# Decoder layer on one core: k's product in two halves around the closing scores, attended rows normalised two tiles at a time

## The chip, the cores and the metric

The kernel runs on one core of a Trainium2 chip. The metric is the time of one execution in microseconds (us), taken on the device. The names of the profile are used throughout: PE is TensorE's matmuls and PEld its weight loads, DVE is VectorE, ACT is ScalarE, POOL is GpSimd, SP is SyncE with its DMA queue. Each engine works through its own list of instructions in order. The engines meet only in semaphores: an instruction adds to one when it is done, and another engine waits until it has reached a count.

## The reference, cut to what matters

```python
# x: [128 sequences, 64 tokens, 128 features], 16 heads of 8 features
x = _layernorm(x + attn(x))            # linear attention and a quantised MLP
x = _layernorm(x + xattn(x, ctx))      # cross attention, the part that the change touches
x = _layernorm(x + ffn(x))             # shared and expert products, top-2 gate

def xattn(x, encoder_output, mask, WQ, WK, WV, WO):
    q = (x @ WQ).reshape(b, s, H, DK).transpose(0, 2, 1, 3)
    k = (encoder_output @ WK).reshape(b, s, H, DK).transpose(0, 2, 1, 3)
    v = (encoder_output @ WV).reshape(b, s, H, DK).transpose(0, 2, 1, 3)
    scores = jnp.einsum('bhqd,bhkd->bhqk', q, k) / SQRT_DK
    scores = jnp.where(masked_or_future, NEG, scores)
    attn = jax.nn.softmax(scores, axis=-1)
    ctx = jnp.einsum('bhqk,bhkd->bqhd', attn, v).reshape(b, s, d)
    return ctx @ WO
```

All of it is float32.

## The kernel before, in words

The 8192 tokens are 64 tiles of 128 rows, in 16 groups of four (`TG` = 4). Three phases follow one another, each a software pipeline over the groups, written out by hand for every engine: linear attention (`phase1`), the MLP (`phase2`), and cross attention with the gated products (`phase3`). The change is in `phase3`. No scheduler and no planner moves anything: the order in an engine's list is the order in which Python calls the helpers.

A step `s` of `phase3` has four slots, `t` = 0 to 3, one for each tile n = 4s + t of group s. Beside that, a step prepares group s + 1 (k, q and v of the context, copied and spread over heads) and finishes group s - 1 (projection of the attended rows, residual, norm, gated products).

What PE does in slot 0, in this order: it transposes tile n's probabilities; does the last gated product of group s - 2; transposes the attended rows of group s - 1 and the x rows of group s + 1; opens the scores of tiles n + 2 and n + 3 (`scores_open`, L1383 and L1394: half of the heads); multiplies tile n's probabilities with v (`weigh_values`, L1455 for an even tile, L1439 and L1446 for an odd one, all into PSUM bank 7); closes the scores of n + 2 and n + 3 (`scores_close`, the same two lines L1383 and L1394, the other half of the heads); and makes k of group s + 1 (`project_qk`, L1464 with `cT,w_xk`, one product of 128x512 into bank 5). Slot 1 follows with the transposes of tile n + 1 (L1427), the projection of the attended rows of group s - 1 (L1229), the q product (L1464 with `yT,w_xq`) and the odd tile's `weigh_values`. Slot 2 begins with transposes and the v product (L1475) and opens the next two tiles' scores.

`scores_close` in slot 0 waits for DVE: the opened half of tile n + 2 must have been read for its maxima (`opened_maxima`, L1040). `scores_open` in slot 2 waits for ACT's copy of the turned probabilities (L793) and for DVE's subtraction of tile n + 3's maxima (L1063), because it writes over the banks that both read.

What DVE does: in slot 0 `opened_maxima`, then `xattend` of tile n (L1030, the reciprocal of 16 sums, and L1032, the product with 128 values). In slot 1 it takes the maxima of the closed half (L1053), subtracts (L1070, two instructions), adds the projection of group s - 1 to x (`residual`, L1127), takes its statistics (L305, L312), and does tile n + 3's maxima and subtraction (L1057, L1063), then `xattend` of tile n + 1. Slots 2 and 3 have one `xattend` each.

`weigh_values` of every tile writes the same columns of bank 7, so it waits on `xatt_ready` until DVE has read the tile before.

## Time and profile before

| what | value |
|---|---|
| time, median of 3 runs (lowest to highest) | 551.51 us (551.32 to 553.45) |
| the profiled execution's own time | 551.02 us |
| its span | 549.3 us |
| busy, share of the span | PE 90%, PEld 67%, DVE 74%, ACT 64%, POOL 68% |

The span is what the profiler covers; the execution's own time is a little more than it. A busy share is an average over the three phases. The page's slices show PE at nine tenths or more in nearly all of the span, and DVE rising from 7 to 8 tenths in the second half, which is `phase3`. TensorE's granted clock is at full speed until the last two slices.

### The profile page before, as it was taken

To read this page: it belongs to the slowest core of one execution; us is meant where nothing else is said; L and a number is where in the kernel's file an instruction comes from. 1 tells how busy PE (TensorE), PEld (TensorE's weight loads), DVE (VectorE), ACT (ScalarE), POOL (GpSimd) and SP (SyncE) were. 2 spreads that over 40 slices of the span, in tenths; PEclk is the share of its full clock that TensorE was granted. 3 is DMA by queue.
4 is the path that set the end of the run, shared out by engine and by line. 5 is a ranking of instruction groups with operands and counts; after the bars stand their busy time and mean duration, and the time that the engine had idled before them with its cause. 6 is when DMAs were issued, how large, how long until landed. Compare 5 with 4: busy or idle time off the path is not lost. (4 is left out here: it accounts for less than half of the span.)

```text
span 549.3 us, 23033 instructions
## 1 busy us (share of the span) xinstructions
PE 495.5 (90%) x9328; PEld 369.2 (67%) x9328; DVE 405.0 (74%) x1410; ACT 354.2 (64%) x649; POOL 372.7 (68%) x685
## 2 busy tenths in 40 slices
PE   2899999998999999998799999999999999999870
PEld 1777777775777777775566767767676666767660
DVE  2777777765777677737577888878888888888866
ACT  1566666656777776764866777666776666767641
POOL 6566666645568785642254888887888878888744
PEclk9999999999999999999999999999999999999987
DMA  6630000000000000001110101211012110120001
GB/s 170 173 118 2 3 2 1 4 2 1 2 0 2 1 2 1 2 2 30 32 33 4 50 8 49 51 51 28 28 52 51 51 31 25 51 51 24 23 2 58
DMA packets 24746, 17.44 MB, mean 32 GB/s; under 512 B 2112, under 2 KB 22464, under 8 KB 24640
## 3 DMA queue, kind: packets, MB, share of 16 engines
q1 hardware_dynamic: 24208, 15.90, 10.5%
q8 instruction: 74, 1.21, 0.9%
q14 instruction: 32, 0.26, 0.1%
q10 hardware_dynamic: 432, 0.07, 0.1%
HBM read 11.77 MB, written 4.19 MB: 29 GB/s over the span
## 5 line engine op out<-in xcount | busy, mean ns | idle before, releaser
L793 ACT ACTIVATE gel<-pair 128x1024 f32<-128x1024 f32 x64 | 51.8, 809 | 40.4 <-PE pair L1427 39.3
L786 ACT ACTIVATE gel<-gel,row_scale 128x512 f32<-128x512 f32 x96 | 66.1, 723 | 18.0 <-DVE gel L1070 15.3
L1369 PEld LDWEIGHTS pair<-w,gel 128*128 128x128 f32 x512 | 60.4, 192 | 8.0 <-issue 5.7
L1369 PE MATMUL pair<-w,gel 128*128 128x128 f32 x512 | 62.5, 276 | 1.0 <-ACT gel L719 1.0
L536 POOL TENSOR_SCALAR k_exp<-k_sb,quad_mask 128x512 f32<-128x512 f32 x64 | 43.2, 694 | 26.9 <-ACT k_sb L766 18.1
L1333 PE MATMUL pair<-hT,w 128*128 128x512 f32 x128 | 58.3, 595 | 1.3 <-ACT lev L714 1.3
L1427 PE MATMUL pair<-ident,gel 128*128 128x128 f32 x384 | 55.3, 280 | 1.5 <-ACT gel L786 1.5
L1427 PEld LDWEIGHTS pair<-ident,gel 128*128 128x128 f32 x384 | 43.3, 141 | 18.4 <-issue 13.5
L1057 DVE TENSOR_REDUCE neg_max<-pair 128x16 f32<-128x512 f32 (+1 forms) x48 | 41.0, 854 | 5.5 <-PE pair L1394 5.5
L1394 PE MATMUL pair<-k_exp,qT 32*32 32x128 f32 (+1 forms) x2048 | 44.3, 333 | 0.0
L513 POOL TENSOR_TENSOR X<-X,proj_sb 128x512 f32<-128x512 f32 x16 | 20.4, 1272 | 35.4 <-ACT proj_sb L677 35.4
L1070 DVE TENSOR_TENSOR gel<-pair,neg_max 128x512 f32<-128x512 f32 x64 | 41.2, 686 | 1.1
L1224 PE MATMUL pair<-ident,xn 128*128 128x128 f32 x192 | 30.5, 283 | 9.6 <-POOL xn L344 9.4
L1333 PEld LDWEIGHTS pair<-hT,w 128*128 128x128 f32 x128 | 22.9, 190 | 24.0 <-issue 23.5
L321 POOL TENSOR_SCALAR veps_b<-mv_b 128x4 f32<-128x4 f32 (+1 forms) x33 | 7.7, 233 | 44.0 <-DVE mv_b L312 25.3
L719 ACT ACTIVATE gel<-lev 128x512 f32<-128x512 int8 x64 | 36.3, 619 | 0.9 <-DVE lev L972 0.9
L1224 PEld LDWEIGHTS pair<-ident,xn 128*128 128x128 f32 x192 | 23.8, 146 | 19.1 <-issue 17.3
L323 POOL TENSOR_TENSOR rstd_b<-veps_b,minus_half 128x4 f32<-128x4 f32 (+1 forms) x33 | 34.5, 1044 | 2.8
L305 DVE BATCH_NORM_STATS2 stats<-X 128x6 f32<-128x128 f32 x128 | 27.6, 279 | 10.5 <-DMA X<-in_x 10.5
L323 POOL TENSOR_TENSOR rstd<-veps,minus_half 128x4 f32<-128x4 f32 x32 | 33.2, 1038 | 2.7
L344 POOL TENSOR_SCALAR xn<-X,negm,rstd 128x128 f32<-128x128 f32 x72 | 31.6, 454 | 3.3 <-POOL negm L339 3.3
L1229 PE MATMUL pair<-w_kv,hT 128*128 128x128 f32 x256 | 33.7, 286 | 0.0
(141 smaller groups left out, 1250.4 us busy)
## 6 DMA issues: line engine op xcount, KB each, us to landing
X<-in_x SPq DMA_DIRECT2D x16, 256.0 KB, 3.1
cT<-in_ctx SPq DMA_DIRECT2D x16, 256.0 KB, 3.9
out_rows<-X SPq DMA_DIRECT2D x15, 256.0 KB, 2.6
mask_rows<-in_mask_early SPq DMA_DIRECT2D x16, 128.0 KB, 3.8
w<-in_L_attn_w SPq DMA_DIRECT2D x2, 256.0 KB, 3.4
out_rows<-X SPq DMA_DIRECT2D x2, 128.0 KB, 1.8
w_kv<-in_L_attn_wk SPq DMA_DIRECT2D x1, 64.0 KB, 3.1
w_q<-in_L_attn_wq ACTq DMA_DIRECT2D x1, 64.0 KB, 2.7
```

The lines of the kernel that those rows point to most:

```text
L323: nc.gpsimd.tensor_tensor(rstd[:, ts], veps[:, ts], minus_half[:, ts], ALU.pow)\
L536: last = nc.gpsimd.tensor_scalar(k_exp[q][:, h, :], k_sb[:, :], quad_mask[:, h:h + 1], 0.0, ALU.mult, ALU.add)
L719: nc.scalar.activation(gel[:, p, f, :], lev[f][:, :], ACT.Gelu_apprx_tanh, scale=QSTEP).then_inc(gel_ready, 1)
L786: nc.scalar.activation(part, part, ACT.Exp, scale=row_scale[:, n:n + 1])\
L793: nc.scalar.activation(pT[par].rearrange("p (a c) -> p a c", a=2), turned, ACT.Copy)\
L1057: nc.vector.tensor_reduce(neg_max[par][:, :].rearrange("p (a h) -> p a h", a=2), scores, AX.X, ALU.max, negate=True).then_inc(max_ready, 1)
L1070: nc.vector.tensor_tensor(rows[:, heads, :], scores[:, half, :, :], neg_max[par][:, heads].unsqueeze(2).broadcast_to([P, HH, S]), ALU.add) ...
L1224: last = nc.tensor.transpose(dst[:, P * t:P * (t + 1)], src[:, t, :], ident[:, :])
L1333: nc.tensor.matmul(bank(up_bank(s, f)), w_1[:, P * f:P * (f + 1)], hT[p][:, :], start=True, stop=True).then_inc(up_done, 1)
L1369: last = nc.tensor.matmul(bank(6 + q)[:, P * t:P * (t + 1)], gel[:, q, f, P * t:P * (t + 1)], w_2[:, f, :], start=(f == 0), stop=(f == NF ...
L1394: last = nc.tensor.matmul(pair[t % 2][b * QW:(b + 1) * QW, quad // 2, heads], qT[p][rows, batch + first:batch + first + QW], k_exp[p][rows ...
L1427: last = nc.tensor.transpose(dst, probability_rows(n)[:, P * i:P * (i + 1)], ident[:, :])
```

## The change

There are two edits.

The first cuts k's product by columns of the context into two products of 128x256. The first half stands in front of slot 0's `scores_close`, with the three waits that the whole product had (`ctx_loaded`, `moe_ready`, `k_ready`); the second half stands behind it, and signals `xk_done`.

The second lets `weigh_values` of an odd tile write into the next 144 columns of bank 7, so that the rows of an even and an odd tile lie side by side. `xattend` then takes a pair: one reciprocal of 32 sums and one product with 256 values, called in slot 1 for tiles 0 and 1 and in slot 3 for tiles 2 and 3, where the odd tile's call stood. Slot 0 and slot 2 have none. `weigh_values` of an odd tile no longer waits on `xatt_ready`; that of an even tile waits for the pair before. In the last group the pair of slots 0 and 1 is joined, and tiles 2 and 3 are done singly as before.

```diff
--- before.py
+++ after.py
@@ -1023,16 +1023,19 @@
                     ln_statistics(dve, ln_a, r, lambda t: X[:, r * TG + t, :], stats_b, mv_b,
                                   ln_a.offs, r * 2)
 
-            def xattend(n, p, t):
+            def xattend(n, p, part):
 
                 dve.wait_ge(pv_done, n + 1)
-                src = bank(7)[:, 0:H * HV].rearrange("p (h e) -> p h e", e=HV)
-                nc.vector.reciprocal(rec[:, 0, 0:H], src[:, :, DH]).then_inc(xrec_ready, 1)
+                count = len(part)
+                src = bank(7)[:, H * HV * (part[0] % 2):H * HV * (part[-1] % 2 + 1)] \
+                    .rearrange("p (h e) -> p h e", e=HV)
+                nc.vector.reciprocal(rec[:, 0, 0:H * count], src[:, :, DH]).then_inc(xrec_ready, count)
                 dve.wait_ge(xrec_ready, n + 1)
-                nc.vector.tensor_tensor(att[p][:, t, :].rearrange("p (h e) -> p h e", e=DH),
-                                        src[:, :, 0:DH],
-                                        rec[:, 0, 0:H].unsqueeze(2).broadcast_to([P, H, DH]),
-                                        ALU.mult).then_inc(xatt_ready, 1)
+                nc.vector.tensor_tensor(
+                    att[p][:, part[0]:part[-1] + 1, :].rearrange("p t (h e) -> p (t h) e", e=DH),
+                    src[:, :, 0:DH],
+                    rec[:, 0, 0:H * count].unsqueeze(2).broadcast_to([P, H * count, DH]),
+                    ALU.mult).then_inc(xatt_ready, count)
 
             def opened_maxima(n):
 
@@ -1149,27 +1152,26 @@
                         gate_top(old, p)
                     if t == 0 and exists(s):
                         opened_maxima(n + 2)
-                        after(dve, xatt_xposed, s - 1)
-                        xattend(n, p, t)
                     if t == 1 and exists(s):
                         shift(n + 1, 0)
                     if t == 1 and exists(prev):
                         residual(prev, 6, range(TG))
                     if t == 1 and exists(s):
                         shift(n + 2, 1)
-                        xattend(n, p, t)
+                        after(dve, xatt_xposed, s - 1)
+                        xattend(n, p, (0, 1))
                     if t == 1 and exists(old):
                         gate_weights(old)
                     if t == 2 and exists(s + 1):
                         future_keys(s + 1, q)
-                    if t == 2 and exists(s):
-                        xattend(n, p, t)
+                    if t == 2 and s == LAST:
+                        xattend(n, p, (2,))
                     if t == 3 and exists(s + 1):
                         shift(n + 1, 0)
                     if s == LAST and t == 3:
                         residual(*halves[0][:1], 5, halves[0][1])
                     if t == 3 and exists(s):
-                        xattend(n, p, t)
+                        xattend(n, p, (3,) if s == LAST else (2, 3))
                     if t == 3 and exists(s + 1) and s >= 0:
                         shift(n + 2, 1)
                     if t == 3 and exists(old) and s < LAST:
@@ -1431,20 +1433,23 @@
             def weigh_values(n, t, p):
 
                 pe.wait_ge(pT_ready, n + 1)
-                after(pe, xatt_ready, n)
+                if n % 2 == 0 or n == NT - 1:
+                    after(pe, xatt_ready, n)
+                first = H * HV * (n % 2)
                 if n % 2:
                     pe.wait_ge(v4_ready, (n // TG + 1) * QB)
                     pe.wait_ge(future_ready, n // TG + 1)
                     for b in range(QB):
                         nc.tensor.matmul(
-                            bank(7)[b * QW:(b + 1) * QW, 0:H * HV],
+                            bank(7)[b * QW:(b + 1) * QW, first:first + H * HV],
                             future[p][:, t // 2, b * QW:(b + 1) * QW],
                             v2[p][:, t // 2 * QB + b, :, :, :].rearrange("p i h e -> p (i h e)"),
                             start=True, stop=False)
                     for i in range(QB):
                         for b in range(QB):
                             last = nc.tensor.matmul(
-                                bank(7)[b * QW:(b + 1) * QW, QB * HV * i:QB * HV * (i + 1)],
+                                bank(7)[b * QW:(b + 1) * QW,
+                                        first + QB * HV * i:first + QB * HV * (i + 1)],
                                 pT[1][:, P * i + b * QW:P * i + (b + 1) * QW],
                                 v4[p][:, t // 2 * QB + b, i, :, :].rearrange("p h e -> p (h e)"),
                                 start=False, stop=i == QB - 1)
@@ -1462,6 +1467,10 @@
             def project_qk(src, w, dst, done):
 
                 nc.tensor.matmul(dst, w[:, :], src[:, :], start=True, stop=True).then_inc(done, 1)
+
+            def project_k_half(q, half):
+                cols = slice(GW // 2 * half, GW // 2 * (half + 1))
+                return nc.tensor.matmul(bank(5)[:, cols], w_xk[:, :], cT[q][:, cols], start=True, stop=True)
 
             def turn_y(g):
                 pe.wait_ge(ln_a.done, g + 1)
@@ -1543,13 +1552,15 @@
                         if n == 0:
                             pe.wait_ge(ysum_ready, NG)
                         weigh_values(n, t, p)
-                    if exists(s) and t % 2 == 0 and n + 2 < NT:
-                        scores_close(n + 2, n + 3)
                     if t == 0 and exists(g):
                         pe.wait_ge(ctx_loaded[q], (g - q) * 8 + 16)
                         after(pe, moe_ready, s * TG - TG)
                         after(pe, k_ready, g)
-                        project_qk(cT[q], w_xk, bank(5), xk_done)
+                        project_k_half(q, 0)
+                    if exists(s) and t % 2 == 0 and n + 2 < NT:
+                        scores_close(n + 2, n + 3)
+                    if t == 0 and exists(g):
+                        project_k_half(q, 1).then_inc(xk_done, 1)
                     if t == 3 and exists(r) and s < LAST:
                         pe.wait_ge(y2T_ready, r + 1)
                         if exists(g):
```

PE's list from a step's slot 0 to the q product of slot 1; the lines are those of each kernel's own file, and a count that is left out is one. Before:

```order
L1394 MATMUL pair<-k_exp,qT 32x128 x8
L1455 MATMUL pair<-v,gel 32x18 x32
L1383 MATMUL pair<-causal_bf,quad_ident 128x256 x2
L1383 MATMUL pair<-causal_bf,quad_ident 128x128 x2
L1394 MATMUL pair<-k_exp,qT 32x256 x8
L1394 MATMUL pair<-k_exp,qT 32x128 x8
L1464 MATMUL pair<-cT,w_xk 128x512
L1427 MATMUL pair<-ident,gel 128x128 x4
L1229 MATMUL pair<-w_xo,attT 128x128 x4
L1464 MATMUL pair<-yT,w_xq 128x512
```

The same place of the changed kernel, on PE:

```order
L1396 MATMUL pair<-k_exp,qT 32x128 x8
L1460 MATMUL pair<-v,gel 32x18 x32
L1473 MATMUL pair<-cT,w_xk 128x256
L1385 MATMUL pair<-causal_bf,quad_ident 128x256 x2
L1385 MATMUL pair<-causal_bf,quad_ident 128x128 x2
L1396 MATMUL pair<-k_exp,qT 32x256 x8
L1396 MATMUL pair<-k_exp,qT 32x128 x8
L1473 MATMUL pair<-cT,w_xk 128x256
L1429 MATMUL pair<-ident,gel 128x128 x4
L1231 MATMUL pair<-w_xo,attT 128x128 x4
L1469 MATMUL pair<-yT,w_xq 128x512
```

The k product (L1464, now L1473) has become two, and the first stands between the weighing of v (L1455, now L1460) and the closing scores.

DVE's list from `opened_maxima` of slot 0 to the attended rows of slot 1. Before:

```order
L1040 TENSOR_REDUCE neg_max<-pair 128x2x4
L1030 RECIPROCAL rec<-pair 128x16
L1032 TENSOR_TENSOR att<-pair,rec 128x128
L1053 TENSOR_REDUCE neg_max<-pair 128x2x4
L1070 TENSOR_TENSOR gel<-pair,neg_max 128x512 x2
L1127 TENSOR_TENSOR X<-X,pair 128x512
L305 BN_STATS stats_b<-X 128x6 x4
L312 BN_AGGR mv_b<-stats_b 128x2 x4
L1057 TENSOR_REDUCE neg_max<-pair 128x16
L1063 TENSOR_TENSOR gel<-pair,neg_max 128x512
L1030 RECIPROCAL rec<-pair 128x16
L1032 TENSOR_TENSOR att<-pair,rec 128x128
```

The same place of the changed kernel, on DVE:

```order
L1043 TENSOR_REDUCE neg_max<-pair 128x2x4
L1056 TENSOR_REDUCE neg_max<-pair 128x2x4
L1073 TENSOR_TENSOR gel<-pair,neg_max 128x512 x2
L1130 TENSOR_TENSOR X<-X,pair 128x512
L305 BN_STATS stats_b<-X 128x6 x4
L312 BN_AGGR mv_b<-stats_b 128x2 x4
L1060 TENSOR_REDUCE neg_max<-pair 128x16
L1066 TENSOR_TENSOR gel<-pair,neg_max 128x512
L1032 RECIPROCAL rec<-pair 128x32
L1034 TENSOR_TENSOR att<-pair,rec 128x256
```

The two instructions between the first two maxima have gone, and the pair at the end has twice the width.

## Rows read from the trace of the kernel before

**Rows 1.** Busy time of `phase3`; after the stretch: its length, busy us (instructions), clock, DMA share, GB/s.

```profile
250.00:530.00 280.00, 259.73 (x6954) 189.15 (x6952) 227.73 (x730) 190.81 (x350) 206.80 (x367) 0.99 0.13 36
```

**Rows 2.** Waits between 300 and 500 us: us in total, times, longest.

```profile
PE pair L1383 <- DVE neg_max L1040: 4.0, 12, 0.3
```

**Rows 3.** PE's timeline in one step: start, us, instructions [idle time before them and releaser].

```profile
393.51 0.28 PE L1383 MATMUL pair<-causal_bf,quad_ident 32*128 32x256 bf16 x4
394.31 0.82 PE L1455 MATMUL pair<-v,gel 128*32 128x18 f32 x64
395.46 0.28 PE L1383 MATMUL pair<-causal_bf,quad_ident 32*128 32x256 bf16 x4 [0.33 <-DVE neg_max L1040]
396.26 1.12 PE L1464 MATMUL pair<-cT,w_xk 128*128 128x512 f32 x2
397.23 0.60 PE L1427 MATMUL pair<-ident,gel 128*128 128x128 f32 x4
398.56 1.02 PE L1464 MATMUL pair<-yT,w_xq 128*128 128x512 f32 x2
399.51 0.45 PE L1439 MATMUL pair<-v,future 128*32 128x144 f32 x8
...
402.53 0.28 PE L1383 MATMUL pair<-causal_bf,quad_ident 32*128 32x256 bf16 x4 [0.16 <-ACT gel L793]
403.33 0.82 PE L1455 MATMUL pair<-v,gel 128*32 128x18 f32 x64
```

**Rows 4.** DVE's timeline in the same step.

```profile
394.62 0.69 DVE L1040 TENSOR_REDUCE neg_max<-pair 128x8 f32<-128x512 f32 x1 [0.29 <-PE pair L1394]
395.25 0.26 DVE L1030 RECIPROCAL rec<-pair 128x16 f32<-128x16 f32 x1
...
396.57 0.69 DVE L1053 TENSOR_REDUCE neg_max<-pair 128x8 f32<-128x512 f32 x1 [0.74 <-PE pair L1394]
397.30 1.29 DVE L1070 TENSOR_TENSOR gel<-pair,neg_max 128x512 f32<-128x512 f32 x2
398.76 0.69 DVE L1127 TENSOR_TENSOR X<-X,pair 128x512 f32<-128x512 f32 x1 [0.17 <-PE pair L1229]
...
401.74 0.69 DVE L1063 TENSOR_TENSOR gel<-pair,neg_max 128x512 f32<-128x512 f32 x1
402.34 0.25 DVE L1030 RECIPROCAL rec<-pair 128x16 f32<-128x16 f32 x1
402.63 0.29 DVE L1032 TENSOR_TENSOR att<-pair,rec 128x128 f32<-128x128 f32 x1
```

**Rows 5.** ACT's timeline in the same step.

```profile
393.21 0.38 ACT L801 ACTIVATE moe_out<-pair 128x263 f32<-128x263 f32 x1
...
401.32 1.02 ACT L793 ACTIVATE gel<-pair 128x1024 f32<-128x1024 f32 x1 [1.10 <-PE pair L1427]
```

**Rows 6.** PE's timeline around the gated products, slot 3 of the step before.

```profile
389.37 0.48 PE L1446 MATMUL pair<-v,gel 128*32 128x36 f32 x32
389.79 1.60 PE L1483 MATMUL pair<-w_moe,y2T 128*128 128x263 f32 x6
391.22 1.04 PE L1427 MATMUL pair<-ident,gel 128*128 128x128 f32 x8
```

**Rows 7.** DVE's groups by form, whole span: line, shapes, count, busy us, mean ns, idle before.

```profile
L1032 DVE TENSOR_TENSOR att<-pair,rec 128x128 f32<-128x128 f32 x64 | 18.7, 292 | 2.2
L1030 DVE RECIPROCAL rec<-pair 128x16 f32<-128x16 f32 x64 | 15.9, 249 | 4.6 <-PE pair L1455 4.2 <-PE pair L1446 0.3
L961 DVE TENSOR_TENSOR att<-pair,rec 128x256 f32<-128x256 f32 x32 | 12.1, 419 | 0.6
L958 DVE RECIPROCAL rec<-den 128x64 f32<-128x64 f32 x16 | 8.9, 553 | 0.5
```

**Rows 8.** PE's timeline, slot 2 of the first and of the last group.

```profile
265.08 0.28 PE L1383 MATMUL pair<-causal_bf,quad_ident 32*128 32x256 bf16 x4 [1.18 <-ACT gel L793]
...
523.64 0.44 PE L1496 MATMUL pair<-ident,att 128*128 128x128 f32 x2 [2.64 <-DVE att L1032]
```

## The prediction, made before the changed kernel had run

> **What bounds the kernel now.** I read the page's slices first, then the busy time by phase, the waits of the middle of `phase3`, and last the timelines of PE, DVE and ACT over one step. In the stretch that holds `phase3` PE is busy for 259.73 of 280 us and DVE for 227.73 [rows 1]: PE is the fullest engine, but both may set the time. The list of waits has PE's wait in front of the closing scores 12 times in 200 us, 4.0 us in all [rows 2], so a step is about 17 us long and loses 0.33 us there. The timeline shows two places in a step at which PE stands still for another engine and that the change can touch [rows 3]: 0.33 us in front of the closing scores of slot 0 (395.46), and 0.16 us in front of the opening scores of slot 2 (402.53).
>
> The second is the one to read closely, since what PE wins in slot 0 has to pass it. The profile puts it down to ACT's L793, which ends at 401.32 + 1.02 = 402.34 [rows 5]. But `scores_open` waits for DVE's L1063 too, and that ends later, at 401.74 + 0.69 = 402.43 [rows 4], 0.10 in front of PE's start. So DVE holds PE there. Where does DVE's list get its time? L1063 stands at the end of an unbroken run: L1053 waits 0.74 us for the closed scores and starts at 396.57, the two L1070 follow, then L1127 with a short wait for PE's projection (398.76), then statistics, maxima and L1063. From L1127's start to L1063's end it is 402.43 - 398.76 = 3.67 us. Hence a loop: closing scores (PE), L1053 to L1070 (DVE), L1127 to L1063 (DVE), opening scores of slot 2 (PE).
>
> How much room has DVE in front of L1127? The two L1070 end at 397.30 + 1.29 = 398.59. A DVE instruction that waits for nothing starts a little before its predecessor's end is written: L1030 at 402.34 against L1063's end at 402.43, so 0.09 earlier. DVE was therefore ready at 398.51 or so, and its room is 398.76 - 398.51 = 0.25 us [rows 4].
>
> **k in two halves: PE's side.** The first half may start when the weighing of v lets go. That ends at 394.31 + 0.82 = 395.13 [rows 3]; after the same narrow tiles a full-width product starts 0.06 before their end (389.37 + 0.48 = 389.85, against 389.79 [rows 6]), so the half starts at 395.07.
>
> What a half costs: float32 makes two passes of each product (x2 where the program has one). The whole k product holds PE from 396.26 to 397.23, 0.97 us [rows 3]. The six passes of 263 columns run from 389.79 to 391.22, 1.43 us [rows 6]. With a first weight load of l and a pass of c per column, l + 2 x 512c = 0.97 and l + 6 x 263c = 1.43; that gives c = 0.83 ns and l = 0.12 us. A half is then 0.12 + 2 x 256 x 0.00083 = 0.54 us, and two halves are 1.09 where one product was 0.97: the second load costs 0.12 us.
>
> There is one more cost, of going from a full-width product to the scores' narrow tiles. The q product, of the same size, starts at 398.56, and its load is hidden behind the projection's products, so its passes take 0.85; the narrow tiles behind it start at 399.51, 0.95 later [rows 3]. That is 0.10 us of change-over. It is paid in front of the closing scores, where before the wait stood.
>
> So the closing scores start at 395.07 + 0.54 + 0.10 = 395.71, plus 0.03 that rounding and their own load leave open: I take 395.73, which is 0.27 later than 395.46. The gap of 0.33 us is more than filled. DVE's maxima are done at 395.31 [rows 4], so that wait no longer holds anything. From the closing scores to the k product it is 396.26 - 395.46 = 0.80; the second half ends at 395.73 + 0.80 + 0.54 = 397.07, and PE is 0.16 us earlier at L1427 than before. That is all that the first edit wins on PE: 0.33 of wait goes, and 0.17 comes back as load and change-over.
>
> The three waits that move ahead with the first half are early: the last of them, ACT's copy of a gated product, ends at 393.59 [rows 5], 1.48 before 395.07. No DMA moves.
>
> A rule of the Trainium skill would make the half cheaper. What the rows show is the first load in the open, 0.12 us. TensorE: Matmul & The Clock Gate (Step-by-step: what each phase is for) says that a weight load is pulled ahead of running matmuls if it goes to the background weight buffer. By it both halves' loads would hide and the closing scores would be 0.15 late and not 0.27; DVE would be ready for L1127 at 398.66, 0.10 before 398.76, and 14 steps would give -1.4 us (a rival below). The rows speak against it, as the whole product has its load in the open at the same change of tiles.
>
> **The same edit: DVE's side.** L1053 follows the closing scores at a fixed distance, so it starts 0.27 later. DVE is ready for L1127 at 398.51 + 0.27 = 398.78. PE's projection, on which L1127 waited, comes 0.16 earlier, so DVE alone decides: L1127 starts at 398.78 against 398.76. All behind it keeps its distance, and L1063 ends 0.02 to 0.03 us later than before. The opening scores of slot 2 move with it, and so does the whole step: PE's 0.16 us are not won, they are added to the wait in slot 2. Per step +0.03 us. Steps 1 to 14 run like this (step 15 has no k product): 14 x 0.03 = +0.4 us. In step 0 the same place waits 1.18 us for ACT [rows 8], whose list begins there with k's copy and may come out up to 0.1 earlier; I count it as nothing.
>
> **Attended rows in pairs.** It turns 64 calls into 33, so 31 fixed costs go, none of them on a path. Bound the pair from both sides. Single: L1030 0.249 and L1032 0.292, with 0.04 between them [rows 4, 7], 0.58 in all. The product with 256 values stands in the trace, with the same kind of operands: L961, 0.419. The reciprocal of 32 does not: it lies between 0.249 (16 values) and 0.553 (64 values, L958) [rows 7]; along the line between them, 0.35. So a pair takes 0.35 + 0.04 + 0.42 = 0.81, 0.23 more than a single one; the ends are 0.13 more (the reciprocal no dearer) and 0.58 more (all doubled).
>
> DVE loses the calls in slots 0 and 2, about 0.5 us each. In slot 0 that is worth nothing: the call stood inside the wait for the closed scores, of which 0.74 was left [rows 4]. In slot 2 likewise, as the maxima behind it wait for PE's closed scores. In slot 1 the pair stands behind L1063, so the loop above doesn't see it. What does wait for it is the even tile's `weigh_values` of slot 2. Before: L1032 ends at 402.63 + 0.29 = 402.92, PE starts at 403.33 [rows 3, 4]. From a DVE end to PE's start 0.15 is needed (L1040's end at 395.31, closing scores at 395.46). The room is 0.26, the pair takes 0.23 of it: it just fits. In slot 3 the pair delays L1057 and L1063 by 0.23; the next to wait is L1040, after 0.29 of idle [rows 4], which still covers it. The odd tile's freed wait is worth nothing either: L1032 of slot 0 ended near 395.84, and PE weighs the odd tile at 399.51.
>
> In the last group nothing covers the pair. PE stands 2.64 us there, waiting for L1032 before it can turn the first attended rows [rows 8], and the rest of the program hangs on that: +0.23 us.
>
> A page of the skill speaks against this edit. Perfetto Trace Analysis (Optimizing Scalar/DVE Operations) says that joining operations helps if the engine is saturated, and that breaking them up may let work finish sooner if it causes bubbles on others. DVE's 0.74 us of idle time per step in front of L1053 puts this case with the second half of that. What it would do here is the third rival.
>
> **Sum.** +0.4 (14 steps) + 0.2 (last group) = +0.6 us on the profiled execution's 551.02, so 551.6. The median of the runs shown is 551.51, 0.5 above it, and the prediction goes by that: 552.1 us.
>
> **Rivals.**
> First, PE is the bound and not DVE: the wait in slot 2 is ACT's, as the profile names it, and ACT moves with PE. For it speaks that ACT's end is only 0.09 before DVE's; against it that DVE's is the later. Then a step wins the 0.16 us: 15 x -0.16 + 0.2 = -2.2, 549.3 us. That is still no change by the measure below.
> Second, the half costs the closing scores nothing (load and change-over vanish in the wait that PE had anyway). Then DVE keeps its start and L1127 follows PE's projection by up to its 0.25 of room: 14 x -0.25 + 0.2 = -3.3, 548.2 us, faster. Against it: the half alone, without load and change-over, is 0.43 us, more than the 0.33 of wait.
> Third, slower: the pair is late for the even tile. If it costs twice a single one, it is 0.58 longer against a room of 0.26, and slot 2 of 14 steps starts its weighing 0.32 late: +4.5, with the sum above 551.5 + 5.1 = 556.6 us. It decides from 0.26 up; by half a percent from about 0.42. For it speaks how little is left (0.03); against it L961, which doubles its width for 0.13.
> Fourth, a half's load does not stand in the open, so that it costs 0.42: 551.5 - 1.4 + 0.2 = 550.3 us. Against it is the whole product's 0.97 [rows 3].
> Fifth, the room in front of L1127 isn't there (DVE's next start needs the end, not 0.09 before it, or the semaphore costs more): per step +0.1 to +0.15, 14 x 0.13 + 0.2 = +2, 553.5 us.
>
> **Numbers.** Two results of this kernel within 0.5% (2.8 us) can't be told apart. The forecast has 0.53, its own range is 551.3 to 553.0. First rival 0.14, second 0.06, third 0.12, fourth 0.05, fifth 0.10. Faster by over 0.5%: the second, and a quarter of the first, 0.09. Slower by over 0.5% (over 554.3): most of the third and a little of the fifth, 0.12. Within: 0.79. The range takes in the first, fourth and fifth rival and leaves out most of the second and third: 549.0 to 554.4.
>
> **What would show it.** In the changed profile the wait in front of slot 0's closing scores is gone; L1464's halves hold PE for some 0.54 us each; the closing scores start about 2.2 us after the opening ones, where it was 395.46 - 393.51 = 1.95; L1053 follows them by 1.11 as before; L1127 no longer waits for PE; and PE's wait in front of slot 2's opening scores has grown from 0.16 to about 0.35, with a step of 17.1 to 17.2 us as before. A step of 17.0 or less would mean that the loop through DVE isn't the bound. A wait of PE for L1034 in front of the even tile's weighing would mean the third rival. A reciprocal of 32 far from 0.35 us would show the step that I interpolated wrong.

## The result, and the profile after

| | before | after |
|---|---|---|
| median of 7 runs each (lowest to highest), us | 552.0 (551.32 to 553.45) | 555.77 (554.76 to 558.05) |
| the profiled execution's own time, its span, us | 551.02, 549.3 | 555.77, 554.1 |

The ratio is 1.0072, with a 95% interval of 1.0058 to 1.0086: slower by 0.7%. The forecast was 552.1 us in a range of 549.0 to 554.4. The time lies above it.

No engine but the weight loads has more to do than before. The busy time of `phase3`, against [rows 1] and with its columns: PE has lost 0.44 us of work and DVE 12.3 us, the weight loads have gained 1.05.

```profile
250.00:530.00 280.00, 259.29 (x6923) 190.20 (x6922) 215.41 (x656) 190.03 (x346) 204.75 (x363) 0.99 0.13 35
```

So look at one step, as the prediction did. PE's timeline of an undisturbed stretch of the changed kernel, from the weighing in slot 0 to slot 2; it answers to [rows 3]:

```profile
396.67 0.82 PE L1460 MATMUL pair<-v,gel 128*32 128x18 f32 x64
397.42 0.70 PE L1473 MATMUL pair<-cT,w_xk 128*128 128x256 f32 x2
398.05 0.28 PE L1385 MATMUL pair<-causal_bf,quad_ident 32*128 32x256 bf16 x4
398.26 0.66 PE L1396 MATMUL pair<-k_exp,qT 32*32 32x256 f32 x32
398.85 0.70 PE L1473 MATMUL pair<-cT,w_xk 128*128 128x256 f32 x2
399.38 0.60 PE L1429 MATMUL pair<-ident,gel 128*128 128x128 f32 x4
...
404.85 0.28 PE L1385 MATMUL pair<-causal_bf,quad_ident 32*128 32x256 bf16 x4 [0.33 <-ACT gel L793]
```

The wait in front of the closing scores (398.05) is gone. A half takes 399.38 - 398.85 = 0.53 us where it is followed by wide work (full-width products), and 398.05 - 397.42 = 0.63 in front of the scores' narrow tiles of 32 columns. The wait in front of slot 2's opening scores has grown from 0.16 to 0.33. DVE in the same step, answering to [rows 4]:

```profile
399.16 0.69 DVE L1056 TENSOR_REDUCE neg_max<-pair 128x8 f32<-128x512 f32 x1 [1.34 <-PE pair L1396]
399.89 1.29 DVE L1073 TENSOR_TENSOR gel<-pair,neg_max 128x512 f32<-128x512 f32 x2
401.09 0.68 DVE L1130 TENSOR_TENSOR X<-X,pair 128x512 f32<-128x512 f32 x1
...
404.67 0.35 DVE L1032 RECIPROCAL rec<-pair 128x32 f32<-128x32 f32 x1
405.12 0.42 DVE L1034 TENSOR_TENSOR att<-pair,rec 128x256 f32<-128x256 f32 x1
```

`residual` (401.09) waits for PE no more. From the weighing of slot 0 to the opening scores of slot 2 it is 404.85 - 396.67 = 8.18 us, against 402.53 - 394.31 = 8.22 in [rows 3]. All that is nearly what was forecast, and no loss is in it.

Where is the loss, then? I cut both traces at the q products (PE's `yT,w_xq`). The lengths are mine, from the starts of these rows:

| us | before | after |
|---|---|---|
| start of the span to step 0's q product | 260.04 | 259.69 |
| the commonest length of a step | 17.12 or 17.13 (9 of 14) | 17.09 to 17.14 (4 of 14) |
| the longest steps | 17.97, 17.84, 17.75, 17.69 | 20.17, 18.12, 18.03, 17.88 |
| the fourteen steps from there | 242.4 | 246.3 |
| last q product to the end | 46.8 | 48.1 |

The loss of the middle stands in single steps. PE's timeline of the worst one, slots 2 and 3 of step 6, of the changed kernel:

```profile
368.57 0.75 PE L1460 MATMUL pair<-v,gel 128*32 128x18 f32 x60
370.81 0.29 PE L1460 MATMUL pair<-v,gel 128*32 128x18 f32 x4 [1.49 <-issue]
371.03 0.39 PE L1385 MATMUL pair<-causal_bf,quad_ident 32*128 32x256 bf16 x4
371.35 1.10 PE L1396 MATMUL pair<-k_exp,qT 32*32 32x256 f32 x32
372.38 1.11 PE L1429 MATMUL pair<-ident,gel 128*128 128x128 f32 x4
```

Two things are to be seen. PE stops for 1.49 us in the middle of a row of 64 like products, none of which has a wait; "issue" says that no semaphore released it. And what comes after runs slower: four transposes take 1.11 us where they take 0.60 to 0.66 otherwise. The page's slices have the granted clock at eight tenths there. In windows (columns as in [rows 1]) the clock is whole before the stop, 0.92 around it, and 0.50, the lower of its two levels (1.2 GHz), in the 3.4 us from 370.90 on, just after PE has gone on:

```profile
361.00:365.00 4.00, 4.00 (x84) 2.67 (x84) 2.76 (x5) 2.54 (x5) 3.82 (x9) 1.00 0.16 45
365.00:372.00 7.00, 5.18 (x208) 3.66 (x193) 4.32 (x19) 3.19 (x5) 6.27 (x11) 0.92 0.41 75
370.90:374.30 3.40, 3.40 (x51) 2.07 (x51) 1.57 (x2) 0.60 (x1) 3.18 (x5) 0.50 0.02 5
```

The last column but one is the other thing that differs: in the second window the DMA engines are busy for 0.41 of the time. They carry the store of a finished group, the mask and the context of a coming one, which SP issues in a row:

```profile
363.48 0.40 SPq L394 DMA_DIRECT2D out_rows<-X  x1
363.92 0.51 SPq L389 DMA_DIRECT2D mask_rows<-in_mask_early  x1
364.47 0.45 SPq L384 DMA_DIRECT2D cT<-in_ctx  x1
```

The same DMA engines carry instructions. The page's third part has them as queues of their own (packets, MB, share); q8 reads the same in both kernels, 16 KB a packet. The second row is the same queue from 360 to 385 us:

```profile
q8 instruction: 74, 1.21, 0.9%
```

```profile
q8 instruction: 5, 0.08, 1.5%
```

I take q8 for PE's supply. Five packets in 25 us are 3.4 in a step of 17.1; PE has 896 records in a step (products, weight loads and waits), so some 260 to a packet, and over the whole span 19058 records to 74 packets, 257.5. The Trainium skill, Runtime: NRT & Kernel Launch (Instruction fetch mechanics), has blocks of 256 instructions, and by that, an estimate, 3.5 a step; it also says that crossing from one block to the next is mostly hidden. The trace agrees with the first. The second is what doesn't hold here.

In the records of this queue a packet runs from 368.39 to 369.37; the data of the three transfers run from 364.41 to 368.43. The packet starts when the data end, PE stops at 369.32, and goes on at 370.81. Two steps later, just behind the undisturbed stretch above, the data end at 404.68, a packet starts at 404.67, and PE stops in the same row again, for less:

```profile
405.69 0.75 PE L1460 MATMUL pair<-v,gel 128*32 128x18 f32 x60
407.02 0.24 PE L1460 MATMUL pair<-v,gel 128*32 128x18 f32 x4 [0.58 <-issue]
```

The kernel before has such a stop too, 0.50 us in the closing scores, in its step of 17.84 us:

```profile
369.12 0.28 PE L1383 MATMUL pair<-causal_bf,quad_ident 32*128 32x256 bf16 x3
369.90 0.21 PE L1383 MATMUL pair<-causal_bf,quad_ident 32*128 32x128 bf16 x1 [0.50 <-issue]
```

Its steps of 17.75 and 17.69 us have no entry for "issue", but a row of 32 products of the closing scores takes 1.29 us (and 1.22 at 473.42) where 0.66 is usual. A halt that is spread over the gaps between short products isn't written as idle time:

```profile
438.54 1.29 PE L1394 MATMUL pair<-k_exp,qT 32*32 32x256 f32 x32
```

One regularity ties all this to q8. I went through the starts of PE's records in all eighteen traces, from 262 to 522 us. In its rows of scores and of weighing there are 60 places where more than 0.35 us lie between one start and the next. At every one of them PE goes on 1.21 to 1.58 us after a packet of q8 has ended; by chance it would be one in thirteen (3.5 packets in 17.1 us, 0.37 us each). In 29 of the 60 that packet had started as the data of a burst ended; in the others the data had ended before it.

Hence the theory that the experiments test (F in the expectations; O and P are its rivals, that the order of the work or the pair itself costs the time): the change shifts, by some instructions per step, where in PE's list a packet of instructions is needed. Where the need falls behind the burst of data and into rows of tiny instructions, which PE goes through fast (64 products in 0.82 us), PE runs dry.

### The profile page after: what moved, and what is told of

Same layout as the page of the kernel before. It is cut to its first block and busy times, and to the rows that moved or that the text cites. A ratio compares the mean times of both kernels' runs of the same rounds, so it can differ in the third digit from the quotient of the medians.

```text
span 554.1 us, 23048 instructions
## 1 busy us (share of the span) xinstructions
PE 499.4 (90%) x9358; PEld 374.1 (68%) x9358; DVE 395.7 (71%) x1348; ACT 355.3 (64%) x649; POOL 371.5 (67%) x685
## 3 DMA queue, kind: packets, MB, share of 16 engines
q8 instruction: 74, 1.21, 0.9%
## 5 line engine op out<-in xcount | busy, mean ns | idle before, releaser
L1226 PEld LDWEIGHTS pair<-ident,xn 128*128 128x128 f32 x192 | 23.9, 146 | 18.9 <-issue 16.9
```

The source lines that it names most:

```text
L1226: last = nc.tensor.transpose(dst[:, P * t:P * (t + 1)], src[:, t, :], ident[:, :])
```

## The experiments

Each is compared with runs of the kernel before on the same chip. "Steps" are the fourteen steps and "tail" what follows the last q product, both of the one profiled execution, to hold against 242.4 and 46.8 before and 246.3 and 48.1 after. A profiled execution may lie one or two microseconds off its median (that of before does by 1.0), so verdicts go by the medians. The diffs are cut to what matters; comments in them are mine.

**One edit at a time.** From after, `xattend` and `weigh_values` as they were before:

```diff
-                        xattend(n, p, (0, 1))
+                        xattend(n, p, t)          # in all four slots
-                if n % 2 == 0 or n == NT - 1:
-                    after(pe, xatt_ready, n)
+                after(pe, xatt_ready, n)
```

> Only k's product in two halves; attended rows tile by tile as before. Theory F (late code): in the changed kernel the undisturbed step is 16.9 to 17.1 us against 17.12, and the 4 us are lost in single steps in which PE stands in the middle of a row of matmuls for lack of instructions, because a refill of its code came behind the burst of data on the queues. By F the undisturbed steps here are 17.1 or less, and the total is 551 to 556, decided by how many steps have a break of 0.5 us or more inside a row of matmuls. Rival O (the order itself): the halves delay the closing scores and with them DVE, evenly in every step: each step 17.3 to 17.4, total 554 to 556, no breaks beyond those of before.

Measured: 553.37 us, ratio 1.0023 (1.0003 to 1.0043); steps 243.8, tail 48.1. Its shortest step is 16.93, and it too has stops, four in the weighing and 2.2 us in all:

```profile
PE pair L1455 <- issue: 2.2, 4, 0.6
```

The other edit alone, `project_qk` for k back in one piece:

```diff
-                        project_k_half(q, 0)
+                        project_qk(cT[q], w_xk, bank(5), xk_done)   # behind scores_close
```

> Only the attended rows in pairs; k's product whole behind the closing scores. F: undisturbed steps 17.12 as before, the last group 0.3 longer, total 551.5 to 553 unless a refill falls badly (then up to 556). Rival O: if the pair is what costs, every step is 0.2 to 0.3 longer with a wait of PE in front of slot 2's weighing, total 555 to 556.

Measured: 555.71 us, ratio 1.0077 (1.0052 to 1.0102); steps 243.4, tail 50.9. The pairs alone cost as much as both edits. In the profile most of it is one stop in step 14, behind which the clock is at its lower level from 513.2 to 516.6:

```profile
512.71 0.43 PE L1396 MATMUL pair<-k_exp,qT 32*32 32x128 f32 x10 [1.50 <-issue]
513.07 0.79 PE L1429 MATMUL pair<-ident,gel 128*128 128x128 f32 x3
```

The packet of q8 in front of it runs from 510.34 to 511.27, and the burst had ended 4.5 us before that: this stop isn't the burst's. The wait for the pair in the last group is 2.9 us here and 2.6 in before and in the halves alone: the pair itself explains 0.3 of 4.0.

**Moving the list without changing it.** 128 semaphore increments at the head of PE's whole list, in after and in before:

```diff
+            for _ in range(128):
+                apart(pe)      # one sem_inc that nobody waits for
```

> The changed kernel with 128 more instructions (semaphore increments that nobody waits for) at the head of PE's list, where PE waits for its first data anyway. They move every later place of PE's list by half a refill (a refill of 16 KB is 256 instructions of 64 bytes). F: the breaks move to other steps and other instructions, and the total changes by over 1 us, most likely down, to 552 to 554, since few placings can be worse than one break of 1.5 us with a fallen clock. Rival O: the same total as the changed kernel within 0.5 us (555.3 to 556.3).

> The kernel before with the same 128 instructions at the head of PE's list. F: the three steps with breaks (17.7 to 17.8 us) move, undisturbed steps stay at 17.12, total 550.5 to 555. Rival O: 552.0 within 0.5.

Measured: 567.31 and 564.77 us, ratios 1.0281 and 1.0236. The increments aren't free as I had taken them to be: their records are 0.15 us apart, PE's first product starts at 20.55 where it started at 9.25 and 9.39, and step 0's q product comes 11.0 and 12.8 us later than without. That swamps the total. The steps can be read all the same: 245.9 (after 246.3) and 242.4 (before 242.4). The stops went to other steps, the 20.17 us step is gone (longest 18.11), and the sum stayed. So a shift of the whole list doesn't undo the loss; inconclusive for the cause.

**Taking the burst away.** Context and mask are loaded for the first two groups only, and later groups use these (in after and in before):

```diff
-                if exists(s + 2):
-                    ...
-                    load_ctx(s + 2, p)
+                if s == -1:
+                    load_ctx(1, p)
```

> The changed kernel, whose context and mask are loaded for the first two groups only and used again for all others (14 loads of 256 KB and 14 of 128 KB are left out); stores and everything else stay. The burst of data in each step shrinks from some 4 us to some 1.5. Theory F (late code): the breaks inside rows of matmuls go or shrink below 0.3 us, every step from 1 to 14 is 16.9 to 17.1 us, total 549 to 551.5, below the same change of the kernel before. Rival O (the order): 4 us above the kernel before with the same change.

> The kernel before with the same loads left out. F: steps 17.12, breaks gone, total 549.5 to 550.5; e5 minus e6 is -1.5 to +0.3. Rival O: 551.5 to 552, e5 minus e6 +4.

Measured: 551.44 us, 0.9983 (0.9969 to 0.9996), and 550.64 us, 0.9975 (0.9961 to 0.9990). PE waits for neither transfer in the kernel before, and yet without them after is 4.3 us faster than it was (0.9% by the two ratios, which allow for the chips), and before 1.4. The difference between the two kernels falls from 3.8 to 0.8.

**Cutting the burst in two.** Nothing is left out; mask and context of a group are asked for half a step later than the store, one group ahead as before:

```diff
-                if exists(s + 2):
+                if exists(s + 2) and s < 1:
...
+                if exists(s + 3) and s >= 0:      # behind the store
+                    sp.wait_ge(future_ready, s + 2)
+                    sp.wait_ge(xv_done, s + 2)
+                    sp.wait_ge(y2_xposed, s + 1)
+                    load_mask(s + 3, 1 - p)
+                    load_ctx(s + 3, 1 - p)
```

> The changed kernel with all its work, but each step's burst of data in two: the store stays in slot 1, the mask's and the context's load wait for slot 3 (y2_xposed), where they are still some 8 us ahead of their use. F: a refill waits at most some 2.5 us instead of 4, the breaks shrink, total 550 to 553.5. Rival O: 555.8 as the changed kernel.

> The kernel before with the same two bursts. F: 550 to 552.5. Rival O: 552.0 within 0.5.

Measured: 551.31 us, 0.9989 (0.9975 to 1.0004), and 549.97 us, 0.9959 (0.9944 to 0.9975). All three transfers are there, 8 us apart, as SP's timeline of the second shows:

```profile
355.68 0.43 SPq L384 DMA_DIRECT2D cT<-in_ctx  x1
364.02 0.40 SPq L394 DMA_DIRECT2D out_rows<-X  x1
372.43 0.33 SPq L389 DMA_DIRECT2D mask_rows<-in_mask_early  x1
372.80 0.43 SPq L384 DMA_DIRECT2D cT<-in_ctx  x1
```

Steps are 241.1 and 241.2, tails 47.9 in both. The list of PE's waits from 250 to 530 us has no entry for "issue" in either, where after had 3.4 us in five, and no row of 32 closing scores takes over 0.69 us; a few steps are still 0.2 to 0.5 us longer than the rest. This is the experiment that carries the explanation: the two edits are untouched, every byte is moved, and 4.5 of after's microseconds are gone. What is left between the kernels, 1.3 us, is twice what the prediction's sum had (0.6); under "The tail" in the next section, 0.66 of it is found. And the kernel before with this edit beats both: 2.2 us faster than before.

**Each edit alone with the burst cut in two:**

> k's product in two halves, attended rows tile by tile, and the burst of data in two (the mask's and the context's load wait for slot 3). Theory F says that what the burst's division leaves is the order's own effect: undisturbed steps 17.09 (in e5 and e7) against 17.12, the last group as before. Expected 549.3 to 550.5, within 0.7 us of the kernel before with the burst in two (549.97). Rival O: 1.5 us or more above that.

> Attended rows in pairs, k's product whole, and the burst of data in two. F: undisturbed steps 17.12, the last group 0.3 us longer for the pair, and DVE's own list with its break in step 14 as in e5 and e7: 550.5 to 552, some 4 us below e2 (555.71). Rival O (the pair costs evenly in every step): 554 or more.

Measured: halves 550.19 us, 0.9964 (0.9946 to 0.9983), the same as before with that edit; pairs 555.34 us, 1.0068 (1.0037 to 1.0099). The first is as expected. The second is a plain miss: pairs alone keep their 3 to 4 us with the burst cut, while pairs and halves together lose it. Its steps are 243.0, 1.8 over before's with the same edit, its tail 48.2. The list of waits has 0.5 us for "issue". The rest is in three rows of closing scores, of 1.34, 1.17 and 0.88 us where 0.66 is usual, 1.4 us too much in all. The first of them, and the same row of before with the cut burst:

```profile
440.14 1.34 PE L1402 MATMUL pair<-k_exp,qT 32*32 32x256 f32 x32
```

```profile
439.31 0.66 PE L1400 MATMUL pair<-k_exp,qT 32*32 32x256 f32 x32
```

From 436 to 442 us the DMA engines carry one packet in that run, that of q8 from 438.68 to 439.64; the last data had ended at 435.76. So PE also runs dry behind a packet that nothing holds up. That accounts for the steps of this profile, not for the whole of the medians' distance: the profiled execution (554.07) is 2.1 us above that of before with the same edit (551.94), the medians are 5.4 apart, and two of its six executions took over 558.

**The tail.** The last group's pair for tiles 0 and 1 taken singly again, on top of the cut burst:

```diff
+                    if t == 0 and s == LAST:
+                        after(dve, xatt_xposed, s - 1)
+                        xattend(n, p, (0,))
```

> The changed kernel with the burst in two, and the last group's tiles 0 and 1 done singly. The pair held PE in the last group 0.31 us longer than the single call did (3.22 against 2.91 us); by that it is 0.2 to 0.4 us below e7 (551.31), 550.8 to 551.2. If the last group's 1.3 us come from elsewhere (a break in DVE's list), no more than that goes.

Measured: 550.94 us, 0.9975 (0.9959 to 0.9990), 0.4 under the one with the pair, where 0.2 to 0.4 was expected. The medians' difference is within the intervals; the profiles bear it out. PE's wait for the attended rows is 2.64 us, where it is 2.94 with the pair and 2.64 in before, and PE turns the rows 21.72 us after the last q product, where it is 22.01 with the pair. The tail as a whole is 48.7, though, not shorter: PE's clock is at its lower level for 6.8 us of it, where it is 3.4 with the pair.

**Is it the burst's time, or its size?** In before, the store, and the loads behind it, held back until the q product is done:

```diff
+                    if exists(s + 2):
+                        sp.wait_ge(xq_done, s + 3)
```

> The kernel before, nothing of the change, with each step's store (and the two loads behind it) held back until the q product of the step is done, some 2 us later, so that the burst lies over slot 2, where PE goes through its instructions fastest. Theory F: PE's refills wait for the end of the burst when they are needed most; breaks of 0.5 us and more inside the rows of slot 2 in half of the steps or more, total 555 to 565. Rival (the breaks have nothing to do with where the burst lies): 552.0 within 1 us.

Measured: 552.22 us, 0.9986 (0.9971 to 1.0002). No change, where 555 to 565 was expected. The data of the burst now begin 1.99 us behind the start of the q product; in before it is 0.0 to 0.4, in after mostly 0.3 to 0.8. So the burst goes past after's place, and being late costs nothing by itself. Its exact place in after isn't tested in this kernel.

**Is it the length of the list?** A steady step has 894 records on PE in before. The halves add four, the pairs take two away (the odd tiles' waits): 898 with halves alone, 892 with pairs alone, 896 in after. Pairs alone, with the odd tile's wait kept as one that is met already (894 again); after with the same wait (898); and before with an added wait, which was meant to give 896:

```diff
-                if n % 2 == 0 or n == NT - 1:
-                    after(pe, xatt_ready, n)
+                after(pe, xatt_ready, n if n % 2 == 0 or n == NT - 1 else n - 1)
```

> Pairs only (as e2), but an odd tile's weighing keeps a wait on xatt_ready, for a count that the even tile has already waited for: it holds nothing back, and gives PE's list the length per step of the kernel before (894 records in the trace where e2 has 892). Theory F, as e10 left it: what e2 loses in its steps is that the refills' places in PE's list move with the length of a step. By F most of e2's 4 us go: 552.0 to 553.5 (the last group's pair and DVE's break stay, about 1 us). Rival P (the pair itself costs): 555 to 556 as e2.

> The changed kernel with that same kept wait: 898 records a step in place of 896. F: the breaks move, and the total changes by 1 us or more, either way; e1 has 898 too and gave 553.37, so 553.5 to 555 with the last group's extra. Rival P: 555.8 within 0.5.

> The kernel before with one more wait for an odd tile's weighing, for a count that was reached long before: two more records a step, 896. F: as the changed kernel's list without its halves and pairs, so breaks in other steps: 552.5 to 556. Rival P: 552.3 within 0.7.

Measured: 554.52 us, 1.0040 (1.0025 to 1.0055); 557.24 us, 1.0086 (1.0062 to 1.0110); 552.06 us, 0.9995 (0.9976 to 1.0014). A wait that is met and holds nothing moves the time of the pairs alone down by 1 to 2 us, and that of after up by 1. In the profile of the first the gain is not in the steps (244.9, against 243.4 without the wait) but in the tail (47.7 against 50.9), where the stop of 1.50 us and the fall of the clock behind it are gone. The steps of the second are 17.8 to 18.5 and 16.9 to 17.3 by turns. The third run tests nothing: its trace has 894 records a step and 371 of waits in all, exactly as before's. Two waits share one record (at 407.07 the new one stands in the record of another of the odd tile's waits), so the list didn't get longer. That it runs as before does, with its slow rows of closing scores in the same two steps, is what the theory has for an unchanged list. So what a few records more or less do is shown, by the first two runs; that the number of records decides it alone isn't. Stops of the second, all in rows without a wait:

```profile
311.87 0.27 PE L1396 MATMUL pair<-k_exp,qT 32*32 32x128 f32 x1 [0.53 <-issue]
...
372.59 0.30 PE L1459 MATMUL pair<-v,gel 128*32 128x18 f32 x10 [0.64 <-issue]
407.72 0.31 PE L1459 MATMUL pair<-v,gel 128*32 128x18 f32 x12 [0.73 <-issue]
```

**DVE's own list.** In step 14 of after DVE stops between `residual` and its statistics, though both are its own work:

```profile
506.32 0.68 DVE L1130 TENSOR_TENSOR X<-X,pair 128x512 f32<-128x512 f32 x1
507.53 0.87 DVE L305 BATCH_NORM_STATS2 stats_b<-X 128x6 f32<-128x128 f32 x4 [0.53 <-DVE X L1130]
```

That idle time is 0.17 in the steps before. A packet of q14, the other instruction queue, starts in that stop, at 507.48. PE's opening scores of slot 2 come some 0.35 us later for it: 4.49 us after the q product in place of the 4.14 of an undisturbed step of after. To move it, 32 increments on DVE in steps 2 to 9 of after:

```diff
+                        if 2 <= s <= 9:
+                            for _ in range(4):
+                                apart(dve)
```

> The changed kernel with 4 more instructions on DVE (increments nobody waits for) in slot 2 of steps 2 to 9, where DVE waits anyway: PE's list is untouched, DVE's places move by 32 until step 9. If the last group's extra (the wait in front of step 14's slot 2 is 0.87 us where the kernel before has 0.35) is a break at the end of a piece of DVE's list, it moves: the tail behind the last q product falls from 48.1 to about 47.6 us, total 555.3. If it is the pair's own, it stays.

Measured: 556.34 us, 1.0071 (1.0043 to 1.0098), tail 48.4. The total and the tail didn't fall: a miss. But the stop itself is gone:

```profile
507.04 0.88 DVE L305 BATCH_NORM_STATS2 stats_b<-X 128x6 f32<-128x128 f32 x4 [0.17 <-DVE X L1130]
```

Slot 2 opens at 4.14 again. The tail is as long all the same because PE's clock is at its lower level for 6.8 us in it, from 527.0, where it is 3.4 in after's. Of the profiles with pairs that of this run alone lacks the stop at this place, and none without pairs has it; so it hangs on where DVE's list stands, which is all that the edit moved. That it is the supply of instructions fits, and is argued.

## Why the prediction was wrong

**The mechanism of the step was right.** Half 0.53 us (0.54 forecast), change-over 0.10 (0.10), no wait in front of the closing scores, `residual` behind DVE alone, slot 2's wait 0.33 (about 0.35), an undisturbed step 17.09 us (17.15). The 0.06 between the last two is all that the sum had too much in a step; over 14 steps it is 0.8 us in favour of the change. "No DMA moves" wasn't quite so: in most steps the burst begins some half a microsecond later against the q product. Of the rivals the fourth had a half at 0.42, by the Trainium skill's TensorE: Matmul & The Clock Gate (Step-by-step: what each phase is for). The trace decides against it here: a half takes 0.53 us (398.85 to 399.38). The first, second and fifth asked for an undisturbed step other than 17.12 by 0.1 or more. The prediction had named a step of 17.0 or less as a sign that DVE isn't the bound, and after has two, 16.89 and 16.96. They don't bear it out. Each follows a long step (18.12, 20.17), whose q product came late, so that slot 2 opens 3.93 and 4.00 us behind it where it is 4.14 in an undisturbed step: a short step gives back what the one before it lost, at most PE's lead of 0.16.

**The pair was slightly mis-sized.** The groups by form, answering to [rows 7]:

```profile
L1034 DVE TENSOR_TENSOR att<-pair,rec 128x256 f32<-128x256 f32 x31 | 13.2, 425 | 3.2
L1032 DVE RECIPROCAL rec<-pair 128x32 f32<-128x32 f32 x31 | 10.8, 348 | 0.0
```

The reciprocal was interpolated right (0.35). Between it and the product lie 405.12 - 404.67 - 0.35 = 0.10 us, where I had carried over 0.04 from the single call. So a pair costs 0.29 more than a single one and not 0.23, over the room of 0.26. The even tile's weighing starts 405.69 - 404.85 = 0.84 behind the opening scores, 0.04 more than the 0.80 of [rows 3], and 0.15 behind the pair's end (405.54), the distance that the prediction had for a wait. So the pair does hold it, by 0.04, and it costs nothing: with pairs alone an undisturbed step is 17.12 or 17.13 as before. The third rival, slower by this wait, and the fifth had the right sign, and neither mechanism is what happened. In the last group, against [rows 8]:

```profile
527.99 0.69 PE L1505 MATMUL pair<-ident,att 128*128 128x128 f32 x2 [2.95 <-DVE att L1034]
```

0.31 us longer, 0.2 forecast. The Trainium skill's page Perfetto Trace Analysis (Optimizing Scalar/DVE Operations) says that breaking instructions up may let work finish sooner where an engine that isn't saturated causes bubbles on others. This place agrees, with its 0.31 us, and the single call put back there took 0.30 off.

**The step that failed is the sum.** "14 x 0.03 = +0.4 us" and "31 fixed costs go, none of them on a path" count what each instruction costs where it stands. They take for granted that PE gets its instructions whenever it is ready for them. It doesn't. The range's upper end, 554.4, had no term for it either, though the prediction's own trace had a stop of 0.50 us at 369.90, rows of closing scores of twice the usual length, and steps of 17.7 to 17.8 among those of 17.12, which I hadn't looked at: I read one clean step and multiplied it.

In numbers: the fourteen steps cost 3.8 us more in the profile. The one step of 20.17 is 3.1 over an undisturbed one. The stop is 1.49 of that; in the 3.4 us at half the clock that follow PE is busy throughout, and half of them is 1.7, by my estimate the rest. From 262 to 520 us the clock falls only twice in the eighteen traces, each time within 0.5 us after PE has gone on from one of the two longest stops (this one, and that of 1.50 with pairs alone). The padded kernel, with the same work and no step over 18.11, has nearly the same sum in more and smaller stops. With the burst cut in two the steps of both kernels are equal (241.1 and 241.2), and the kernels differ by 1.3 us by their medians.

**The tail** is 1.3 us longer, and PE's records behind the last q product tell where. 0.16 is no loss: the q product itself comes that much earlier in a kernel with halves, and the span's first part is shorter for it. 0.35 is DVE's stop in step 14, 0.31 the pair. By then, when PE turns the last group's first attended rows, after is at 22.04 and before at 21.15. The other 0.4 lies behind that, in a part where the clock falls in every profile, and it stays open. What the clock does there differs from profile to profile: the lower level holds for 3.4 us in some and 6.8 in others, and of the kernels with single calls and whole k the first have tails of 46.8 (before, before padded, before with the added wait), the others 47.6 to 47.9. The halves alone have 6.8 us of it, so their 48.1 is no sign of a cost. Tails can only be compared where the clock was down for as long.

**What is shown, and what stays open.** Shown: in after as it is, 4.3 to 4.5 us hang on the context and mask transfers landing together with the store, though nobody waits for them. That it goes by way of PE's instruction packets rests on the place of the stops, in rows that wait for nothing, on PE going on 1.21 to 1.58 us after a packet's end at all 60 places, and on the long stops going when the burst is cut; no run changed the packets alone. Shown as well: the burst isn't the only way to run dry. With pairs alone the longest stop, 1.50 us, and the slow rows with the burst cut stand behind packets that no data held up, and this is why cutting the burst doesn't help there. Not settled: how much of the +3 to +4 us of pairs alone it is (a wait that holds nothing brings back a third to a half of the loss), and what decides when a packet is asked for. A run that puts the packets' borders at chosen places without taking PE's time would tell; increments cost too much for that.

## What to carry to other kernels

Before multiplying one clean step, lay all steps side by side and explain the longest: here the spread of 0.7 us among the steps of before was larger than any term of the sum. Where a list has hundreds of tiny instructions per step, look for idle time put down to "issue" inside a row of like instructions, and for rows that take longer than their like; it says that the supply of instructions is a resource, and that any edit of the list, even one that is faster in every step, may move the time by several microseconds either way. Ask for bulk transfers away from such rows and away from each other, even where nobody waits for them: here that was worth 0.4% of the kernel before, more than either edit.

## What the runs showed of the hardware that I hadn't expected

- A stop of 1.49 us on PE cost 3.1: the clock was at its lower level, 1.2 GHz, from 370.9 to 374.3, and four transposes took 1.11 us where 0.60 to 0.66 is usual.
- At all 60 breaks of more than 0.35 us inside PE's rows of scores and of weighing it went on 1.21 to 1.58 us after a packet of q8 had ended.
- A semaphore increment on PE that nobody waits for took 0.15 us; 128 of them put the first product off from 9.25 to 20.55.
- Two waits that stand next to each other in PE's list shared one record, so that an added wait left the number of records at 894 a step.
- DVE's product behind a reciprocal of 32 values started 0.10 us after its end, and behind one of 16 values 0.04.
